# One exponential per head worked out by the Vector engine, and the loads and stores of a head put in another order

## The reference

```python
s1 = einsum('bhqd,bhkd->bhqk', q1, k1) * scale      # s2 likewise from q2, k2
a1 = softmax(where(causal, s1, -inf));  a2 = softmax(where(causal, s2, -inf))
out = einsum('bhqk,bhkv->bhqv', a1 - lam * a2, v)
normed = (out - mean(out)) * rsqrt(var(out) + 1e-5)
x = layernorm(x + merged(normed * (1 - LAM_INIT)) @ Wo)
x = layernorm(x + w3(gelu(h2(gelu(h1(silu(w1 x) * (w2 x)))))))
```

## Time and profile before

| | |
|---|---|
| runs | 1888.0 us median of 3 (1886.88 to 1888.72) |
| profiled execution | 1887.07 us, its span 1885.1 us |
| mean granted clock | 0.997 |
| busy, share of the span | PE 98%, ACT 75%, PEld 56%, DVE 55%, POOL 12% |
| attention stage | from 150.4 us to about 1163 us of the span |

### The profile page before, as it was taken

One profiled execution on the slowest core, in us unless ns is written; L12 is line 12 of the kernel. 1 busy time (PEld: TensorE's weight loads), 2 busy tenths in 40 slices (PEclk: granted clock), 3 DMA queues, 4 the chain that ended last, 5 costly groups with the idle time before them and its releaser, 6 DMA issues.

```text
span 1885.1 us, 30736 instructions
## 1 busy us (share of the span) xinstructions
PE 1851.2 (98%) x12160; PEld 1060.2 (56%) x12160; DVE 1030.8 (55%) x2005; ACT 1408.2 (75%) x1702; POOL 232.2 (12%) x308
## 2 busy tenths in 40 slices
PE   7999999999999999999999999999999999999997
PEld 6774333333333333333333335888888888888886
DVE  5566556555655665566556655454545454636343
ACT  4448999999999999999999997444545454545452
POOL 3002111211121112111211121000000000000000
PEclk9999999999999999999999999999999999999999
DMA  8878246634663466346633721000010101000000
GB/s 265 275 250 163 45 85 118 104 71 80 118 107 66 81 118 110 65 79 118 123 55 76 118 61 43 26 12 34 12 34 12 34 12 34 12 34 23 1 12 14
DMA packets 130192, 146.10 MB, mean 78 GB/s; under 512 B 74276, under 2 KB 100516, under 8 KB 122404
## 3 DMA queue, kind: packets, MB, share of 16 engines
q1 hardware_dynamic: 128456, 139.31, 34.1%
q10 hardware_dynamic: 1584, 4.72, 0.8%
HBM read 101.79 MB, written 39.06 MB: 75 GB/s over the span
## 4 chain that ended last, share of the span: by engine, by line
PE 92%; DVE 5%; issue 1%; DMA 1%; ACT 0%; ACTq 0%; SPq 0%; DVEq 0%; PEldq 0%
PE attn_sums_ps L1060 27%; PE split_hid_ps L1664 25%; PE attn_s_ps L1035 20%; PE split_hid_ps L1648 6%; PE proj_qk_ps L526 3%; PE split_y_ps L1681 3%; PE proj_v_ps L536 2%; PE split_y_ps L1604 2%; PE attn_sums_ps L1068 2%; PE split_turn_ps L1592 1%; DVE attn_raw L1206 1%; DVE attn_raw L1195 1%; DMA proj_wv_low_raw<-in_wv 1%; DVE attn_sums_sb L1190 0%; DVE attn_diff L1211 0%
## 5 line engine op out<-in xcount | busy, mean ns | idle before, releaser
L1005 ACT ACTIVATE attn_probs<-attn_s_ps 128x1024 f32<-128x1024 f32 x1088 | 1002.6, 1128 | 8.0 <-PE attn_s_ps L1035 7.4
L1060 PE MATMUL attn_sums_ps<-attn_probs,heads_v 128*32 128x512 f32 (+3 forms) x5120 | 587.3, 540 | 0.0
L1035 PEld LDWEIGHTS attn_s_ps<-heads_q,heads_k 50*128 50x128 f32 x2560 | 211.9, 184 | 436.9 <-ACT attn_probs L1005 402.7
L1035 PE MATMUL attn_s_ps<-heads_q,heads_k 50*128 50x512 f32 (+3 forms) x2560 | 449.8, 425 | 1.7 <-ACT attn_probs L1005 1.7
L1758 ACT ACTIVATE split_whole<-split_hid_ps,scales 128x512 f32<-128x512 f32 x128 | 88.3, 690 | 274.5 <-PE split_hid_ps L1664 274.3
L986 POOL TENSOR_SCALAR_AFFINE_SELECT attn_probs<-attn_probs 128x512 f32<-128x512 f32 x256 | 179.5, 712 | 830.6 <-ACT attn_probs L1005 830.6
L1664 PE MATMUL split_hid_ps<-split_hid_b,ffn_r 128*128 128x512 f32 x1024 | 240.8, 392 | 0.0
L1664 PE MATMUL split_hid_ps<-split_hid_a,ffn_r 128*128 128x512 f32 x1024 | 238.0, 391 | 0.0
L1664 PEld LDWEIGHTS split_hid_ps<-split_hid_a,ffn_r 128*128 128x128 f32 x1024 | 190.1, 188 | 41.0 <-DVE split_hid_a L1933 0.6
L1664 PEld LDWEIGHTS split_hid_ps<-split_hid_b,ffn_r 128*128 128x128 f32 x1024 | 189.8, 188 | 38.2
L1060 PEld LDWEIGHTS attn_sums_ps<-attn_probs,heads_v 128*32 128x32 f32 x5120 | 107.6, 108 | 174.2 <-issue 141.1
(11 more groups left out here) (174 smaller groups left out, 1665.7 us busy)
## 6 DMA issues: line engine op xcount, KB each, us to landing
heads_q_raw<-qk_raw SPq DMA_DIRECT2D x60, 384.0 KB
heads_k_raw<-qk_raw SPq DMA_DIRECT2D x60, 384.0 KB
qk_raw<-proj_copies SPq DMA_DIRECT2D x64, 256.0 KB, 2.4
values<-proj_v SPq DMA_DIRECT2D x8, 1024.0 KB, 6.3
heads_k_raw<-ones SPq DMA_DIRECT2D x60, 128.0 KB
heads_v<-values SPq DMA_DIRECT2D x15, 512.0 KB, 19.0
heads_spare<-in_ffn SPq DMA_DIRECT2D x30, 256.0 KB, 9.9
diffs<-attn_diff SPq DMA_DIRECT2D x30, 256.0 KB, 4.1
```

What stands on the lines that cost most here:

```text
L1005: nc.scalar.activation(weights, side_by_side, ACT.Exp, scale=SCALE).then_inc(exp_done, 1)
L1035: last = nc.tensor.matmul(s_ps[(NU * h + n) % SLOTS][:, s, col:col + width], k_sb[u][rows, b * SEQ + j * PARTS:b * SEQ + (j + 1) * PARTS], ...
L1060: last = nc.tensor.matmul(sums[c * D:(c + 1) * D, off:TILE], v_sb[u][:, b * KEY_BLOCKS + j, :], probs[k % PROBS][:, b, s, place:place + wi ...
```

## The change

1. For heads 0 to 14, unit 39 (`SOFT_UNIT`: step 21, key block 0 of tile 3, batch 0) is not done by ACT. DVE takes the 1024 scores out of PSUM scaled (`soft_take`) and works out the exponential in eight passes over 128x1024 f32 elements in SBUF (`soft_passes`: passes 0 and 2 are tensor_scalar, the six others scalar_tensor_tensor). PE's scores of unit 42, which use the same slot, wait for `soft_taken`.
2. `weigh` of step 21 then has batch 1's two matmuls only; batch 0's two are done by `weigh_soft`, behind the weigh of step 34, which PE reaches in step 1 of the next head.
3. The buffers of these passes lie in the place of the last three weight chunks. Six weight halves are therefore loaded and rounded in the last head (`load_pair`, `round_pair`), through the free values buffer; the other 24 in heads 0 to 12, one after `square_heads`, one after `copy_sums` of tile 3.
4. SP issues the next stacks when the scores of the head before are done, then values, then the fourth tile's rows of the head before (`store_rest`), a half, the rows of tiles 0 to 2 (`store_ahead`), a half.
5. The pieces are cut in the order of the query tile that needs them; PE waits for 6, 8, 12 and 16 of 16 by tile. DVE cuts five before `soft_take` and eleven after tile 2.
6. ACT's and POOL's attention programs stand in two branches of a flag, as PE's and DVE's did.

```diff
+    SOFT = END[2] + 1
+    SOFT_AT = END[3] - 1
+    SOFT_UNIT = UNITS.index((SOFT, [0]))
-        WIDE_AT = END[1] + 2
+        WIDE_AT = END[2]
-        CUT_ORDER = [(name, piece) for piece in range(PIECES) for name in ("k", "q")]
+        PIECE_ORDER = [(0, 0), (0, 1), (1, 0), (1, 1), (0, 2), (1, 2), (0, 3), (1, 3)]
+        CUT_ORDER = [(name, b * QUERY_TILES + t) for b, t in PIECE_ORDER for name in ("k", "q")]
@@ sync_program
+                    if not first:
+                        sp.wait_ge(scored, NU * h)
                     load_shift(...)
                     for b in range(BATCH):
                         load_stacks(...)
+                    sp.wait_ge(probs_free, PROBS + NS * h)
                     sp.dma_start(v_sb[1 - u][:, :, :], values[h + 1]).then_inc(values_loaded[1 - u], 16)
+                    if not first:
+                        store_rest(h - 1)
+                load_next_half(2 * h)
+                store_ahead(h)
+                load_next_half(2 * h + 1)
@@ tensor_program
+                    if nn == SOFT_UNIT and has_soft(hh, exact):
+                        pe.wait_ge(soft_taken, hh + 1)
+            def weigh_soft(h, u):
+                pe.wait_ge(soft_passed, SOFT_PASSES * (h + 1))
+                for s in range(2):
+                    nc.tensor.matmul(sums_ps[STEPS[SOFT][0] % 2][s * D:(s + 1) * D, :], v_sb[u][:, STEPS[SOFT][1][0], :], soft[:, bass.ts(s, TILE)], start=False, stop=False)
@@ vector_program, last_head
+                round_pair(0)
                 copy_sums(h, 1)
                 early_rstd()
...
                 early_norm(3)
-                for s in range(2):
-                    early_heads(s)
-                    early_add(s)
+                round_pair(1)
+                early_heads(0)
+                early_add(0)
+                early_heads(1)
+                round_pair(2)
+                sum_counts()
+                early_add(1)
@@ vector_program
+            def head_with_soft(h):
+                tile(h, 0)
+                square_heads(h)
+                round_next(2 * h - 1)
+                tile(h, 1)
+                cut_stacks(h + 1, u, range(0, 5))
+                soft_take(h)
+                soft_passes(h, range(0, 4))
+                copy_sums(h, 2)
+                soft_passes(h, range(4, 7))
+                take_turned(h, 2)
+                finish_tile(h, 2)
+                soft_passes(h, range(7, SOFT_PASSES))
+                cut_stacks(h + 1, u, range(5, CUTS))
+                copy_sums(h, 3)
+                round_next(2 * h)
+                take_turned(h, 3)
+                finish_tile(h, 3)
```

More of the change, by code:

```diff
@@ L125, in _ @@
             exact = project["load_exact"](pool)
+            with pool.If(exact == 0):
+                attention["gpsimd"](pool, False)
             with pool.If(exact != 0):
                 maximum["gpsimd"](pool)
-            attention["gpsimd"](pool)
+                attention["gpsimd"](pool, True)
         @block.scalar
@@ L132, in _ @@
             project["scalar"](act)
-            attention["scalar"](act)
+            exact = project["load_exact"](act)
+            with act.If(exact == 0):
+                attention["scalar"](act, False)
+            with act.If(exact != 0):
+                attention["scalar"](act, True)
         @block.tensor
@@ L841, in laid, with has_soft, unit_done, begins_sums @@
         return places
+    def has_soft(h, exact):
+        return not exact and h < LAST
+    def unit_done(h, exact, n):
+        if exact:
+            return NU * h + n + 1
+        return (NU - 1) * h + n + 1 - (has_soft(h, exact) and n > SOFT_UNIT)
+    def begins_sums(h, exact, k, b):
+        t, blocks = STEPS[k]
+        if has_soft(h, exact) and t == STEPS[SOFT][0] and b == 0:
+            return k == SOFT + 1
+        return blocks[0] == 0
     CORNERS = [[place for j, _, _, place in laid(k) if j >= SUBS * STEPS[k][0]] for k in range(len(STEPS))]
@@ L848, in attention_programs @@
         stage = spare[:, 1, :].bitcast(F32)
+        late_stage = v_sb[LAST % 2 - 1][:, :, :].rearrange("p (a k) d -> p a (k d)", a=2)
+        soft, whole_part, power = (whole_w[:, KEPT_CHUNKS + n, :] for n in range(3))
         probs = [room.sb(f"probs{n}", [PARTS, BATCH, 2, TILE]) for n in range(PROBS)]
@@ L1025, in scores @@
                     pe.wait_ge(values_loaded[u], 16 * ((h + 1) // 2))
-                    pe.wait_ge(cut_done, TAIL + CUTS * h)
+                if blocks[0] == 0 and batches[0] == 0 and not first:
+                    pe.wait_ge(cut_done, TAIL + CUTS * (h - 1) + CUTS_UP_TO[t])
                 if not first or n >= SLOTS:
-                    pe.wait_ge(exp_done, NU * h + n - SLOTS + 1)
+                    hh, nn = (h, n - SLOTS) if n >= SLOTS else (h - 1, NU + n - SLOTS)
+                    if nn == SOFT_UNIT and has_soft(hh, exact):
+                        pe.wait_ge(soft_taken, hh + 1)
+                    else:
+                        pe.wait_ge(exp_done, unit_done(hh, exact, nn))
                 for i, b in enumerate(batches):
@@ L1056, in weigh @@
                 for j, off, width, place in laid(k):
-                    for b in range(BATCH):
+                    for b in range(1, BATCH) if k == SOFT and has_soft(h, exact) else range(BATCH):
                         for s in range(2):
@@ L1111, in use @@
                 weigh(h, u, k)
+                if k == SOFT_AT and has_soft(h, exact):
+                    weigh_soft(h, u)
                 if k - TURN_LAG in END:
@@ L1168, in round_half @@
                 k, cols = half_chunk(n)
-                dve.wait_ge(w_loaded, 16 * n + 16)
+                stage = half_stage(n)
+                if n >= KEPT_HALVES and n % 2 == 0:
+                    dve.wait_ge(w_loaded, 16 * n + 32)
+                else:
+                    dve.wait_ge(w_loaded, 16 * n + 16)
                 nc.vector.tensor_copy(rounded[:, k, cols], stage).then_inc(w_rounded, 1)
@@ L1394, in vector_program @@
+            for h in range(LAST):
+                if has_soft(h, exact):
+                    head_with_soft(h)
+                else:
+                    head_of_all(h)
             last_head(LAST)
```

152 lines of the change are left out of this document (107 added, 45 removed).

## The result

| | before | after |
|---|---|---|
| median of runs (lowest to highest) | 1888.1 us (1886.9 to 1889.7) | 1896.6 us (1893.5 to 1899.2), 6 runs |
| ratio after to before | | 1.0044, 95% interval 1.0033 to 1.0054 |
| profiled execution | 1887.07 us, span 1885.1 | 1899.07 us, span 1897.0 |
| mean granted clock | 0.997 | 0.994 |

The change costs 0.44%. The time lies inside the stated range (1879 to 1899), but that is no merit of the sum, which said +0.8 us: the range is wide enough to hold the rivals. "No change that can be told", the likeliest case, was wrong: the time is of rival B's kind, a late take. The profiled execution is 12.0 us over that of before, 3.5 more than the medians are apart, so what follows from one profile is sized again by the medians of the experiments. T is, as in the prediction, the time at which PE starts the scores of step 21.

The account below looks back on a forecast made before the run. ACT's exponentials were taken as the bound, PE close behind; -8.5 + 7.3 - 0.5 + 2.5 = +0.8 us on the profile's 1887.1, 1888.8 on the median's scale; range 1879 to 1899.

Parts of the forecast that it names:

- No change that can be told: Whole kernel: time within about 0.2% (3.8 us) of before; chance of same 0.44.
- rival B: Heads 1 to 12: batch 1's stacks land late, delaying DVE's take; 1 us gives 1901, two 1913; chance 0.16.
- ACT's 0.917 an exponential: Attention on ACT: each further exponential in a row costs 0.917 us; one fewer in 15 heads, 13.8 us if all showed.
- the bubble of 0.35: Step 22: ACT waits 0.35 us for PE's scores where unit 39 was, leaving -0.57 per soft head, -8.5 us in all.
- The late weigh at 0.9: `weigh_soft` in step 1 on PE: two matmuls take 0.9 us, between bounds of 0.5 and 1.0.
- Rival A: PE less in the way: two matmuls cost about half, or the late weigh falls into a wait; 1880 to 1883; chance 0.29.
- C's 1.0: Rival in which PE pays more: 1.0 us for the late weigh and 5 us in the last head, 1893; chance 0.12.
- What it does to a head: Steps 2 to 12: the late weigh costs each head behind a soft one 0.5 us; head periods of 62.4 to 62.6.
- DVE's passes: DVE, each head: take, passes and gaps of 10.7 to 11.4 us, hidden; tensor_scalar between 0.9 and 1.23, take 1.2 to 1.4.
- When the take can start: Step 21: batch 1's stacks in at 624, fifth cut done at 625.3, scores there at 625.7; another 0.7 us late costs nothing.
- The last head at +2.5: Last head: 1.65 us of the second pair's roundings and 0.9 of the stored rows' late load show, together +2.5 us.
- The first head's branch at 0: First head: ACT's new branch costs 0 (to +1), because PE does the same wait and branch beside it.

Follow-up runs that it names:

- e6: e3's kernel with the late weigh's two matmuls left out, so part of tile 3's sums is missing: 1877.8 us, ratio 0.9952.
- e1: The changed kernel with four cuts, not five, before DVE's take: 1892.2 us, ratio to before 1.0021.
- e4: e3's kernel with the late weigh behind step 26's weigh, not step 34's, and all eight passes before the take of tile 2's turned sums: 1882.8 us.
- e2: The changed kernel with the last head's stored rows loaded ahead of the second pair of weight halves, second and third pairs rounded later: 1897.5 us.
- e3: The changed kernel with the edits of e1 and e2 together: 1887.8 us, ratio to before 1.0000.
- e5b: e3's kernel with ACT doing all 68 exponentials of every head, without DVE's passes and the late weigh: 1887.7 us, ratio 0.9996.
- e7: e3's kernel with 2, 3, 4 and 5 more DVE passes ahead of the take in heads 3, 6, 9 and 12: 1899.8 us, one execution.

## Why the prediction was right or wrong, point by point

- **ACT's 0.917 an exponential, the bubble of 0.35**: right (e6: 62.46 - 0.56 = 61.90).
- **The late weigh at 0.9**: 0.84 measured. The Trainium skill (TensorEngine Tiling (Array Packing), Key Properties) has tiles run in parallel; the trace agrees so far that two matmuls cost most of what four do (0.84 against 0.99) and not half. Rival A, which took half, is out, and so is C's 1.0.
- **What it does to a head**: 62.54 against the 62.5 forecast. ACT's losses lie in the steps that were named. This chain, by which only the bound and PE's lead in each step count, held to 0.05 us.
- **DVE's passes**: tensor_scalar took 0.69, below the lower end of 0.9 that twice a 512 cast gave; the take took 1.22. All hidden, as said; e1 to e4 show no wait for any pass.
- **When the take can start**: this is the step that failed. The forecast had the half ahead of the stacks issued at T - 29.0 us and the last stack in 27.9 later, with 0.7 to spare until it costs. The issue came at T - 28.8, and the room was right: a landing 0.7 later, 0.25 late at the take, cost nothing in head 7. But from that issue to the landing it took 27.4 us in head 5, 27.9 in head 10, 28.4 in head 7 and 29.9 in head 1, whose last piece came at T + 1.04 (249.59 - 248.55). The median of heads 1 to 12 is 29.0. So the 27.9, built from the time of one head, was 1.1 us short of the middle, and the scatter of 2.5 us about it was put at nothing. Where the scatter comes from, the runs do not show. The rival's price (one us for each) was right up to 2 us, and the clock's share on top of it was missing.
- **The last head at +2.5, and 0.3 for the late weigh**: 5.7 measured. The load's wait was 1.62, inside the 0 to 1.9 given. The term for the second pair's roundings (1.65) did not show as such, the first pair, put at nothing, cost up to 0.85 (e2's wait that is left), the late weigh 0.65 in place of 0.3, and the clock took 2.7 that no term had. With e2's order 1.4 is left.
- **The first head's branch at 0**: 62.8 against 63.4 before; but 64.0 to 65.5 in e1, e3, e4, e5b and e7. It goes with a stretch at half clock at 153 to 155 us: none in e2 (head 0: 62.6), 3.4 us in after and e6 (62.8), 6.8 in e1 and e7 (64.0), 10.2 in e3, e4 and e5b (65.1 to 65.5). No edit of the experiments changes what runs before 184 us, so it is a matter of the execution, and up to 2.5 us of any comparison of two profiles is this.
- **Chances**: 0.44 on no change came from treating "just in time" as in time. Room of 0.7 us behind a 28 us transfer, twelve heads over, should have made the late take the likeliest case.

## What to carry to other kernels

Work moved from the bound engine to an idle one is worth the time saved less what it puts back on the engine close behind the bound. Here this was all of it (e5b), until the added work was put where that engine has a lead (e4: 0.3% faster). Before a new wait is costed at nothing, hold its room against the times of the transfer in all repetitions, not in one. And move the consumer behind the wait, not the transfer, if one order of the same work has 2.7 us of room and the other 0.7.

## What was not expected of the hardware

A short stall of PE can cost more than itself. Six waits of PE in attention were 1.60 to 3.48 us long: in head 1 and the last head of after, in the last head of e1, in head 12 of e2 and in heads 9 and 12 of e7. With each of them TensorE's granted clock went from full to half (2.4 to 1.2 GHz level) for 3.4 or 6.8 us, from 0.9 us ahead of the wait's end to 0.9 us behind it, at a price of 1.6 to 3.0 us on top of the wait. With its waits of 0.65 to 1.09 us it did not. The runs show the stretches, not what decides them; the one at 153 to 155 us, where attention starts, has no such wait beside it.
